# A recurrent block with routed experts: a split wait for a tanh, two more banks in the first step, new orders of the instructions

## The reference

```python
xn = layernorm(x)
# time mix, 4 heads of 64 channels
dx = shift_by_one_token(xn) - xn
mix = tanh((xn + dx * x_miu) @ x_A)              # 6 groups of 32
miu = lambdas + einsum('btgk,gkc->gbtc', mix, x_B)
r_in, w_in, k_in, v_in, a_in, g_in = xn + dx * miu
v, r = v_in @ vW.T, r_in @ rW.T
g = tanh(g_in @ g_A) @ g_B
w = -softplus(-(w_miu + tanh(w_in @ w_A) @ w_B)) - 0.5
k = normalized(k_in @ kW.T + tanh(k_in @ k_A) @ k_B)
a_gate = 2 * sigmoid(a_time + a_in @ a_A @ a_B)
# per head and token:  sa = S a;  S = S*decay + sa b^T + v k^T;  y = S r
y = wkv7(r, w, k * exp(min(w / 2, 0)), v, -k, k * a_gate)
s = ((groupnorm(y) * gamma + beta) + sum(r * k * x_time) * v) * g @ oW.T
# feed forward: 2 of 8 experts by a softmax, each expert is wi plus a low-rank part
f = sum_e gate_e * (relu(xn @ wi.T + bi + (xn @ lora_A[e].T) @ lora_B[e].T) @ wo.T + bo)
out = x + s * silu(f)
```

## Time and profile before

| | us |
|---|---|
| median of 3 runs | 993.72 (992.63 to 994.07) |
| the profiled execution, its own time | 996.0 |
| its span, first to last instruction | 993.9 |
| PE busy | 977.4 |
| DVE busy | 834.8 |
| ACT busy | 635.9 |
| POOL busy | 442.7 |

### The profile page before, as it was taken

How to read it: one execution, slowest core, us unless ns; L and a number is a source line. 1 busy time by engine, 2 the same in 40 slices (tenths; PEclk the granted TensorE clock), 3 DMA queues, 4 the chain that set the end, 5 groups by cost and what they waited for, 6 DMA issues and landing times.

```text
span 993.9 us, 46770 instructions
## 1 busy us (share of the span) xinstructions
PE 977.4 (98%) x20578; PEld 769.6 (77%) x20578; DVE 834.8 (84%) x1684; ACT 635.9 (64%) x1481; POOL 442.7 (45%) x537
## 2 busy tenths in 40 slices
PE   8999999999999999999999999999999999999997
PEld 5777778787787877778777787877878777777775
DVE  5887979789798897979979797887988979799775
ACT  4665666757757566676656667576575666756564
POOL 3461724537254371633627245372443716346250
PEclk9999999999999999999999999999999999999999
DMA  7000000000000000000000000000000000000000
GB/s 260 13 3 3 3 4 23 4 23 4 13 13 4 23 4 23 4 3 24 4 23 4 3 24 3 23 4 3 23 4 24 3 24 3 3 24 4 13 4 23
DMA packets 9416, 17.28 MB, mean 17 GB/s; under 512 B 1920, under 2 KB 4224, under 8 KB 8960
## 3 DMA queue, kind: packets, MB, share of 16 engines
q1 hardware_dynamic: 9216, 14.30, 4.4%
HBM read 10.10 MB, written 4.19 MB: 14 GB/s over the span
## 4 chain that ended last, share of the span: by engine, by line
PE 95%; ACT 2%; DVE 1%; issue 1%; SPq 0%; DMA 0%; ACTq 0%; DVEq 0%
PE bank L255 34%; PE bank L254 20%; PE grams L470 10%; PE bank L348 5%; PE bank L496 3%; PE bank L485 2%; PE grams L539 2%; PE grams L444 2%; PE grams L594 2%; PE grams L559 2%; PE bank L570 2%; PE bank L363 2%; PE bank L379 2%; PE bank L529 2%; PE bank L580 2%; PE bank L303 1%
## 5 line engine op out<-in xcount | busy, mean ns | idle before, releaser
L1265 POOL TENSOR_TENSOR bk<-bk,tot 128x256 f32<-128x256 f32 x192 | 154.8, 814 | 139.8 <-PE grams L470 139.8
L1583 DVE COPY_PREDICATED gm<-c_mask_g,grams 128x1024 f32<-128x1024 int32 x96 | 161.4, 1682 | 5.3 <-PE grams L470 3.0
L1021 ACT ACTIVATE gl<-gm 32x128 f32<-32x128 f32 x320 | 99.1, 310 | 74.6 <-DVE gm L1583 68.2
L914 ACT ACTIVATE relu<-bank,prm 128x256 f32<-128x256 f32 x256 | 105.8, 472 | 39.8 <-PE bank L255 35.2
L1246 POOL TENSOR_TENSOR xd<-mtmp,xnc 128x512 f32<-128x512 f32 x96 | 122.3, 1276 | 14.1 <-DVE mtmp L1449 12.4
L470 PEld LDWEIGHTS grams<-ar,bk 64*64 64x64 f32 x6144 | 102.4, 134 | 22.1 <-issue 15.4
L255 PE MATMUL bank<-w_wo,hid 128*128 128x256 f32 x488 | 116.1, 386 | 0.0
L470 PE MATMUL grams<-ar,bk 64*64 64x64 f32 x6144 | 110.7, 220 | 2.1 <-DVE ar L1593 1.2
L1593 DVE TENSOR_TENSOR ar<-ar,tot 128x512 f32<-128x512 f32 x96 | 92.6, 965 | 12.3 <-PE grams L470 12.3
L255 PEld LDWEIGHTS bank<-w_wo,hid 128*128 128x128 f32 x488 | 90.2, 190 | 13.1
L1449 DVE SCALAR_TENSOR_TENSOR mtmp<-bank,prm,dx 128x256 f32<-128x256 f32 x192 | 80.8, 478 | 16.7 <-PE bank L348 16.7
(11 more groups left out here) (239 smaller groups left out, 2149.3 us busy)
## 6 DMA issues: line engine op xcount, KB each, us to landing
x_in<-x SPq DMA_DIRECT2D x16, 256.0 KB, 2.8
out<-out_t SPq DMA_DIRECT2D x15, 256.0 KB, 2.0
w_wi<-w_wi_dram SPq DMA_DIRECT2D x1, 1024.0 KB, 6.8
w_wo<-w_wo_dram SPq DMA_DIRECT2D x1, 1024.0 KB, 9.1
w_lora_B<-w_lora_B_dram SPq DMA_DIRECT2D x1, 512.0 KB, 8.5
w_x_B<-w_x_B_dram SPq DMA_DIRECT2D x1, 384.0 KB, 3.4
w_kW<-w_kW_dram SPq DMA_DIRECT2D x1, 256.0 KB, 4.2
w_rW<-w_rW_dram SPq DMA_DIRECT2D x1, 256.0 KB, 4.0
```

What stands on the lines that cost most here:

```text
L914: A(dst[:, p % 2, j * 256:(j + 1) * 256], ZB[p % 2][:, j * 256:(j + 1) * 256], ACT.Relu, bias=prm[:, P_BI + 2 * p + j:P_BI + 2 * p + j + 1 ...
L1021: A(gl[l % 2][o:o + 32, :, :, :].rearrange("p q g (c n m) -> p (q g c) n m", c=2, m=m), right(gm[o:o + 32, :, :, :, b, 0, 32 * k:32 * k + ...
L1265: tt(v, v, d, ALU.mult).then_inc(S(f"bk{k}_scaled"), 1)
L1583: run(v.copy_predicated(dst, msk.to_broadcast([128, 32, HALF // m, m]), src), "g_stored")
```

## The change

It has four parts.

1. `mixt_e` is cut in two, `mixt_e` (the large tanh) and `mixt_f` (the four small ones), and `miu(pair)` waits for `mixt_done` 1 for pairs 0 and 2 and for 5 for pair 1. In a full step both calls stay together, and PE waits for 5 ahead of `miu(0)` as before.
2. In the first step the second pair of mixes goes to banks 0 and 2 (`mixes_in`), and the bank tables are dealt out anew.
3. The first step has new orders on all engines. The tanhs stand ahead of the routing work on ACT, `route` and `kW` move behind on PE, there are 20 warm matmuls (5, 6, 3, 1, 1, 1, 3) where there were 17 (5, 1, 1, 2, 3, 2, 3), and the sum of the first mix is made by DVE (`mixed_sum(0)`) instead of POOL.
4. The full step, which step 2 shares, has new orders on all engines, with other waits for the banks. `route`, `r_` and `v_` lose `half=True`; `diff(3)` and `down(0)` gain it.

The last step keeps its order; two waits for copies change names. Not in the core below: ACT's orders (in step 1 the tanhs stand right behind `xnc_e`, ahead of `rt_e` and `exps`) and the first half of DVE's full step (`hidden(1)` moves from behind `first_expert` to ahead of `store(1)`, `mixed(5)` and the scalings move by a place or two). The core of the diff:

```diff
+def mixes_in(pair):
+    return (bank[0], bank[2]) if steps["front"] == 0 and pair == 1 else MIU
...
 def miu(pair):
-    pe.wait_ge(*till("mixt_done", 5))
+    pe.wait_ge(*till("mixt_done", 5 if pair == 1 else 1))
     for c in range(2):
         for o in (0, 64):
             for k in range(2):
                 r, u = 64 * k, pair % 2
-                last = mm(MIU[k][o:o + 64, c * 256:(c + 1) * 256], w["x_B"][r:r + 64, pair, c * 128 + o:c * 128 + o + 64],
+                last = mm(mixes_in(pair)[k][o:o + 64, c * 256:(c + 1) * 256], w["x_B"][r:r + 64, pair, c * 128 + o:c * 128 + o + 64],
                           mixt[r:r + 64, u, :], start=True, stop=True)
...
     if step == 2:
         pe.wait_ge(*till("mx_4_done", 0))
         pe.wait_ge(*till("mx_5_done", 0))
-        pe.wait_ge(*till("xmt_done", 0))
+        pe.wait_ge(*till("v_done", 0))
         pe.wait_ge(*till("bonus_done", 0))
     if step == 1:
         warm(5)
     if step == 1:
         if front:
             xt_()
-            warm(1)
-            route()
-            warm(1)
+            warm(6)
             mix()
-            warm(2)
+            warm(3)
             if step == 1:
                 wait_loaded(pe, 1)
             miu(0)
-            warm(3)
+            warm(1)
+            pe.wait_ge(*till("xnc_done", 1))
+            pe.wait_ge(*till("mixt_done", 5))
+            miu(1)
+            route(half=True)
+            warm(1)
+            wk_A()
+            kW(half=True)
+            pe.wait_ge(*till("mx_2_done", 2))
+            wk_B()
+            wait_loaded(pe, 2)
+            pe.wait_ge(*till("mx_3_done", 2))
+            a_A()
             pe.wait_ge(*till("mx_0_done", 2))
             pe.wait_ge(*till("mx_1_done", 2))
-            miu(1)
-            kW(half=True)
-            wk_A()
-            wait_loaded(pe, 2)
-            pe.wait_ge(*till("xnc_done", 1))
-            g_A(half=True)
+            miu(2)
             pe.wait_ge(*till("route_read", 1))
-            wk_B()
-            pe.wait_ge(*till("mixt_done", 5))
-            a_A()
-            pe.wait_ge(*till("mx_2_done", 2))
-            pe.wait_ge(*till("mx_3_done", 2))
-            miu(2)
+            g_A()
+            pe.wait_ge(*till("hwk_done", 1))
+            a_B()
             pe.wait_ge(*till("kraw_done", 1))
             pe.wait_ge(*till("ksq_done", 1))
-            a_B()
-            pe.wait_ge(*till("hwk_done", 1))
             norm()
-            warm(2)
-            pe.wait_ge(*till("hg_done", 1))
+            warm(1)
+            pe.wait_ge(*till("sig_done", 2))
             r_()
-            pe.wait_ge(*till("sig_done", 2))
-            v_()
             pe.wait_ge(*till("ha_done", 1))
             g_B()
+            pe.wait_ge(*till("hg_done", 1))
+            xmt_()
             pe.wait_ge(*till("agate_done", 2))
-            xmt_()
+            v_()
             warm(3)
             pe.wait_ge(*till("nrm_done", 1))
             bonus_()
             pe.wait_ge(*till("r_done", 1))
-            pe.wait_ge(*till("gate_done", 1))
+            pe.wait_ge(*till("xmt_done", 1))
             diag(rec)
...
             base(0)
         if front:
             if full:
+                pe.wait_ge(*till("xmt_done", 0))
+            xt_()
+        if rec:
+            lora(0)
+            diff(1)
+        if front:
+            if full:
                 pe.wait_ge(*till("gate_done", 0))
-            xt_()
-        if rec:
-            diff(1)
-            lora(0)
+            route()
+        if rec:
             gram(1)
         if front:
-            if full:
-                pe.wait_ge(*till("xmt_done", 0))
-            route(half=True)
             pe.wait_ge(*till("xnc_done", 1))
             mix()
         if rec:
+            base(3, half=True)
             diff(0, half=True)
-            base(3, half=True)
+            gram(2)
         if front:
             if step == 1:
                 wait_loaded(pe, 1)
...
             pe.wait_ge(*till("route_read", 1))
             miu(0)
         if rec:
-            gram(2)
+            lora(3)
+            base(2)
             inv_x(1)
-            base(2)
-            lora(3)
-            inv_off(1)
         if front:
             pe.wait_ge(*till("mx_0_done", 2))
             pe.wait_ge(*till("mx_1_done", 2))
             miu(1)
         if rec:
             gram(3)
-            inv_x(2)
+            inv_off(1)
         if front:
             pe.wait_ge(*till("mx_3_done", 2))
             wk_A()
         if rec:
-            lora(2, half=True)
-            inv_off(2)
+            diff(3, half=True)
+            inv_x(2)
         if front:
             pe.wait_ge(*till("mx_2_done", 2))
             pe.wait_ge(*till("hwk_done", 1))
             miu(2)
         if rec:
+            down(1, first=True)
+            inv_off(2)
             gram(4)
-            diff(3)
         if front:
             pe.wait_ge(*till("mx_4_done", 2))
             kW()
...
             pe.wait_ge(*till("kraw_done", 1))
             pe.wait_ge(*till("ksq_done", 1))
             g_A()
+            pe.wait_ge(*till("sig_done", 2))
+            norm()
+        if rec:
+            inv_off(4)
+        if front:
+            pe.wait_ge(*till("hg_done", 1))
+            a_A()
+        if rec:
+            lora(2, half=True)
+            top_x()
+            rec_p(0)
+            top_off()
         if post:
             if front:
-                pe.wait_ge(*till("sig_done", 2))
+                pe.wait_ge(*till("nrm_done", 1))
             elif full:
-                pe.wait_ge(*till("xmt_done", 0))
+                pe.wait_ge(*till("gate_done", 0))
             zt_()
-        if rec:
-            inv_off(4)
-        if front:
-            pe.wait_ge(*till("hg_done", 1))
-            norm()
-        if rec:
-            down(1, first=True)
+        if front:
+            pe.wait_ge(*till("ha_done", 1))
+            r_()
+        if rec:
             if post:
                 pe.wait_ge(*till("zt_done", 1))
             elif front:
-                pe.wait_ge(*till("sig_done", 2))
+                pe.wait_ge(*till("nrm_done", 1))
             elif full:
-                pe.wait_ge(*till("xmt_done", 0))
+                pe.wait_ge(*till("gate_done", 0))
             keys_to_tokens(0)
-            top_x()
-            rec_p(0)
-            top_off()
-        if front:
-            pe.wait_ge(*till("nrm_done", 1))
-            r_(half=True)
-            if rec:
-                pe.wait_ge(*till("bkt_done", 1))
-            elif post:
-                pe.wait_ge(*till("zt_done", 1))
-            else:
-                pe.wait_ge(*till("sig_done", 2))
-            a_A()
-        if rec:
             rec_sa(0)
             y_state(0)
-            diff(2, half=True)
-            rec_inc(0)
         if front:
             pe.wait_ge(*till("r_done", 1))
             a_B(half=True)
         if rec:
             rec_y(0)
-            rec_p(1)
-            down(0)
-            rec_sa(1)
-            y_state(1)
-        if front:
-            pe.wait_ge(*till("ha_done", 1))
-            bonus_()
-        if rec:
-            if front:
-                pe.wait_ge(*till("agate_done", 2))
-            elif full:
-                pe.wait_ge(*till("gate_done", 0))
-            keys_to_tokens(1)
-            rec_y(1)
+            rec_inc(0)
         if post:
-            if front:
-                pe.wait_ge(*till("bonus_done", 1))
-            elif rec:
+            if rec:
                 pe.wait_ge(*till("bkt_done", 1))
             else:
                 pe.wait_ge(*till("zt_done", 1))
             o_(half=True)
         if rec:
-            rec_inc(1)
-        if front:
-            if rec:
-                pe.wait_ge(*till("bkt_done", 2))
-            else:
-                pe.wait_ge(*till("agate_done", 2))
-            v_(half=True)
-            diag(rec)
-        if rec:
-            down(3)
-            down(2, final=True)
-        if front:
+            rec_p(1)
+        if front:
+            pe.wait_ge(*till("agate_done", 2))
+            bonus_()
+        if rec:
             if post:
                 pe.wait_ge(*till("o_read", 1))
             else:
-                pe.wait_ge(*till("bonus_done", 1))
+                pe.wait_ge(*till("bkt_done", 1))
+            keys_to_tokens(1)
+            rec_sa(1)
+            y_state(1)
+            diff(2, half=True)
+            rec_y(1)
+            down(0, half=True)
+            rec_inc(1)
+        if front:
+            diag(rec)
+            pe.wait_ge(*till("bonus_done", 1))
+            v_()
+        if rec:
+            down(2)
+            down(3, final=True)
+        if front:
+            if rec:
+                pe.wait_ge(*till("bkt_done", 2))
+            elif post:
+                pe.wait_ge(*till("o_read", 1))
+            else:
+                pe.wait_ge(*till("nrm_done", 1))
+            g_B()
+            pe.wait_ge(*till("v_done", 3))
             xmt_()
```

(87 more changed lines are left out.)

108 lines of the change are left out of this document (54 added, 54 removed).

## The result

The changed kernel takes 999.39 us (median of 4 runs, 998.65 to 1000.26) against 993.89 us for the kernel before on the same chip: ratio 1.0054, 95% interval 1.0042 to 1.0066. It is slower by 0.54%, outside the predicted range (989.9 to 998.2) and on the side that the prediction gave a chance of 0.26. The profiled execution of the changed kernel took 998.65 us, its span is 996.8.

The account below looks back on a forecast made before the run. The prediction took PE, busy throughout a full step, to bound the kernel. List -0.3, gaps +1.0, step 2 -1.0, first step -0.8 and added waits +0.7 summed to -0.4 us: 993.3 us, range 989.9 to 998.2.

Parts of the forecast that it names:

- What bounds the kernel: PE is busy throughout a full step; other engines' work costs nothing there until it makes PE wait.
- The matmul list: Full step on PE: tile form changes priced for both orders, -0.02 us a step, -0.3 us over 14 steps.
- The added waits: Full step: PE waiting for other engines in the new order, 0.05 us a step, +0.7 us (0 to +5.6).
- The slower rival: End of a full step: DVE, held by POOL, reaches the barrier before gram(0) late; 998.2 us, chance 0.26.
- the forecast case: Whole kernel: likeliest outcome, 993.3 us, with DVE's 0.81 us idle time taking up y1's lateness; chance 0.29.
- The instruction gaps: Full steps: PE runs out of instructions where 256 are used up quickly; two more such stretches, +1.0 us (-2 to +4).
- Step 2: Step 2: the 1.28 us gap before the second state increment goes, smaller waits come; -1.0 us (-1.6 to 0).
- The first step: First step: earlier tanhs, new banks and DVE's sum bring miu(0), wk_A and diag earlier; -0.8 us (-1.3 to 0).
- it doesn't do what it says: Rival for the first step: DVE's queue eats the gain, -0.8 becomes 0; 994.1 us, chance 0.12.
- The sum: Whole kernel: -0.3 + 1.0 - 1.0 - 0.8 + 0.7 = -0.4 us, 993.3 us for the median.

Follow-up runs that it names:

- e4: The kernel before with POOL's scale_bk(3, 1) moved ahead of mixed(2), nothing else: 992.85 us, ratio 0.9989.
- e12: The changed kernel, PE's order untouched, with POOL, DVE and ACT operations reordered to remove waits at gram(3), top_off and rec_inc(0): 995.02 us, ratio 1.0013.
- e6: The changed kernel with down(1) directly ahead of kW, POOL's scale_bk(2, 1) and scale_bk(3, 1) and DVE's scale_ar(3) moved forward: 1003.10 us, ratio 1.0089.
- e11: The kernel before with 64 waits on a long-past event ahead of PE's first matmul: 998.17 us, ratio 1.0041.
- e9: e4's full step with the changed kernel's first step, its DVE and ACT orders mended and warm(1) for warm(3) ahead of miu(0): 992.69 us, ratio 0.9988.
- e2: The changed kernel with the first step of the kernel before: 1000.28 us, ratio 1.0061.
- e7: The changed kernel with DVE's keep_top ahead of first_mask: 999.20 us, ratio 1.0046.

## Why the prediction was wrong, step by step

**What bounds the kernel** was right: PE, in both orders, with no idle time of PE in a full step without gaps.

**The matmul list** was mis-sized. Predicted -0.02 us a step. Without any wait the old list takes 59.99 (e4), the new one 60.11 (e12): +0.12 a step, 1.7 us. Against it the old wait went, 1.3 us in 13 steps, so that this term is +0.4 us instead of -0.3. The 0.2 us for a block put alone among smaller forms was right (e6). What failed is the exit from `miu(2)`: I had priced entries into and exits from 128\*128, and took a 64\*64 block to be left for nothing, 0.91. Leaving it costs 0.11 us, and between two other forms it takes 1.02. The step ahead of the change had that number already, at `wk_B`, which stands between 32\*32 blocks and takes 1.02; I read it as that block's own length. Against it, `zt_` came out 0.05 cheaper than priced.

The 0.09 us ahead of `gram(4)` I counted as part of the old list. It was a wait for POOL (e4), and it went with the new order, as a gain that something else then ate.

**The added waits** are the step that failed most: +0.05 a step was taken, and 0.32 came in a step that has all three. Over the 14 steps `gram(3)` cost 1.6 us, `rec_inc(0)` 1.4 and `top_off`, in 7 of them, 0.8: 3.7 us instead of 0.7. It lies inside the range I gave for this term (0 to 0.4 a step). Of the narrow places that I named, `rec_inc(0)` was one, with 0.2 us of margin in my placing and -0.10 in truth. The other two, `store(2)` ahead of `gram(3)` and `keep_top` ahead of `top_off`, I had not named: I had looked at the scalings that a gram reads, and not at the mask copy that frees its bank. All three are smaller than my placing error, 0.2 to 0.3; the prediction said that its margins were too, and yet took nearly the bottom of the range. With half a dozen places each near zero margin, it is unlikely that what is late adds up to nearly zero.

**The slower rival** had the right sign and the wrong place. DVE is not late at the barrier ahead of `gram(0)`: in the changed kernel base(1) takes 1.822 us there, before 1.820. `y1` starts 0.7 us later in the step than before, and this was covered, as the forecast case had it. The full step is longer than 60.2 in all its copies, as this rival's sign asked, but without the idle time ahead of `gram(0)`, `gram(2)` or `down(2)` that belonged to it. So a time near 998.2 would not have confirmed the mechanism.

**The instruction gaps**: predicted +1.0, measured 4.9 against 4.8 us in 14 steps in this pair of traces, and 5.3 against 4.2 as means over six traces of either order. The mechanism held (e11), and the size agrees with the means. Since single traces scatter by 0.9, that the size came so near is partly luck, and no one pair could have shown it.

**Step 2**: predicted -1.0, measured -0.14. The 1.28 us gap went, the 0.5 us gap near 68 did not come back, and the 0.6 us for `rec_p(1)` came as forecast (0.60). But `norm`, earlier in the new order, now waits for ACT's `sig` (0.34 us idle, and the block ahead of it 0.5 longer), and the terms of the full step come on top.

**The first step**: predicted -0.8, measured -0.2 from the copy `xnc` on. `miu(0)` came 5.43 behind the copy against 5.90, a gain of 0.47 (0.65 predicted), and `wk_A` and `nrm` came earlier too; but `key_norm` starts at 28.11 where it could at 27.70, behind `mixed(5)` and the masks held by POOL's sums. That is the rival "it doesn't do what it says" for this part, as far as 0.2 us can be told from it. e9 got 0.56 more from the same edit with the queues mended and two warm-up matmuls less, so the gain was there to be had.

**The sum**: the list without the old wait +0.4, the new waits +3.7, the gaps +0.2, step 2 -0.1, the first step -0.2: +3.9 us by this pair of traces (rounded), and +4.9 with the mean difference of the gaps, 1.1, in place of 0.2. The medians differ by 5.5, with 1.2 on either side; e2 alone gives 6.1 (4.5 to 7.6). So the terms reach the measured time within its interval.

## What to carry to other kernels

In an order where one engine is busy all the time, list for every block not only the inputs that it reads but also what frees the bank that it writes, and add up what a margin below the error of placing costs on average, instead of taking such margins as held. A wait of 0.05 to 0.1 us shows in no idle time: look at whether the weight loads of a block start ahead of its first matmul, and compare the same block's start-to-start time with its neighbours' forms. Undoing single swaps on the other engines is the cheap test, and here it gave two versions (e4, e9) whose medians are 0.1% below the kernel before, with intervals that end just under 1. And the excess over the shortest step is no measure of the gaps where the shortest step holds waits that a gap would hide.

## What the runs showed of the hardware that was not expected

- Leaving a block of 64\*64 tiles for another form costs 0.11 us and entering it 0.05, with 256 columns (0.91 entered, 0.98 left, 1.02 both) as with 64 (0.98, 1.04, 1.09); entering and leaving 128\*128 costs 0.20 in all (e6). The Trainium skill ("TensorEngine Tiling (Array Packing)", Key Properties) gives the drain, without a size.
- PE stops at number 193 modulo 256 of its own records, with 0.55 to 1.2 us between the starts of two records in the 49 largest cases, mostly where 256 records are used up within 2.8 us (39 of 49), and goes on 1.22 to 1.61 us after the end of a packet of the instruction queue (14 traces); shifting the program by 32 records moves the places (e11).
- A swap that shortens the shortest full step by 0.11 us left the median unchanged (e7): the wait that it takes away was there in 7 of 14 steps only, and the gaps differ from run to run by about as much. Below 0.2% the step, and not the time, is what tells.
- In one execution (the profiled one of before) the granted clock of the last step was 0.95 instead of 1.00, and that step took 1.5 us longer. The clock was at its lower level, 1.2 GHz, from 971.9 to 975.3 us; the block of 8 matmuls of `diff` that took 1.97 us there took 1.08 in the changed kernel. PE had waited 0.67 us for ACT just before, in both kernels alike.
- The start of the copy `xnc` varied from 7.07 to 7.78 us between kernels that are the same up to there.
